# An empty indirect gather on GpSimd ahead of the first tile's gather, in an attention and routed-expert kernel

## What is computed

```python
x = x + xattn(layernorm(x), ctx)     # 16 heads of 16, keys from context and x, causal on x
x = x + ffn(layernorm(x))

def ffn(x):                          # T = 2048 tokens, E = 8 experts, cap = T // E
    probs = softmax(xt @ Wg)
    _, top_idx = top_k(probs.T, cap)             # each expert takes its 256 best tokens
    # a token taken by several goes to the best of these, one taken by none to its best expert
    tok2exp = where(assigned, argmax(masked), argmax(probs.T))
    for e in range(E):
        out += where(tok2exp == e, weight, 0) * (gelu(xt @ W1[e]) @ W2[e])
```

## Time and profile before

| | us |
|---|---|
| median of three runs | 372.68 (372.06 to 373.13) |
| the profiled execution | 371.51 |
| its span, first to last instruction | 369.5 |
| TensorE busy | 350.9 |
| ScalarE busy | 264.4 |
| VectorE busy | 207.4 |
| GpSimd busy | 126.3 |
| mean granted TensorE clock | 0.993 of full |

### The profile page before, as it was taken

The page is one execution under the profiler, slowest core; times in us unless marked ns, Lnnn a source line. Parts: engine busy times, 40 slices in busy tenths (PEclk is TensorE's granted clock), DMA queues, the critical chain, the costliest instruction groups (busy, mean ns, idle before and its releaser), DMA issues.

```text
span 369.5 us, 11056 instructions
## 1 busy us (share of the span) xinstructions
PE 350.9 (95%) x4371; PEld 224.8 (61%) x4371; DVE 207.4 (56%) x711; ACT 264.4 (72%) x386; POOL 126.3 (34%) x222
## 2 busy tenths in 40 slices
PE   8999999999999999999999999998786799999995
PEld 7757547444434444444434344787665799999994
DVE  4999797454546455454635456697785233333332
ACT  3675564999999999999999999307851445555440
POOL 6445768001010313131120306504404346555523
PEclk9999999999999999999999999999999899999999
DMA  7634899505366563826565125401652321323200
GB/s 246 192 106 138 248 249 324 175 4 150 73 197 159 186 171 92 249 45 179 129 180 126 35 35 182 134 2 64 217 179 63 103 86 58 110 70 93 70 26 33
DMA packets 37374, 47.83 MB, mean 129 GB/s; under 512 B 8780, under 2 KB 26626, under 8 KB 37313
## 3 DMA queue, kind: packets, MB, share of 16 engines
q1 hardware_dynamic: 34368, 40.26, 37.3%
q0 software_dynamic: 2608, 6.43, 5.6%
q10 hardware_dynamic: 337, 0.32, 0.3%
HBM read 32.84 MB, written 13.81 MB: 126 GB/s over the span
## 4 chain that ended last, share of the span: by engine, by line
PE 79%; ACT 9%; DVE 7%; issue 3%; POOL 1%; POOLq 0%; ACTq 0%
PE ps L1189 20%; PE ps L1165 18%; PE ps L1412 10%; PE ps L1426 9%; PE ps L1143 8%; ACT pbuf L912 7%; PE ps L1089 4%; DVE stats L1794 1%; PE ps L1058 1%; ACT v_st L962 1%; PE ps L1400 1%; DVE xe L1789 1%; PE ps L1282 1%; POOL pbuf L789 1%; PE ps L1072 1%
## 5 line engine op out<-in xcount | busy, mean ns | idle before, releaser
L912 ACT ACTIVATE pbuf<-ps 128x948 f32<-128x948 f32 (+2 forms) x192 | 167.5, 1028 | 0.1
L1758 DVE SCALAR_TENSOR_TENSOR pbuf<-pbuf,seen 128x128 f32<-128x128 f32 (+1 forms) x256 | 70.9, 309 | 65.6 <-ACT pbuf L912 64.8
L1165 PE MATMUL ps<-q_st,k_st 98*32 98x512 bf16 (+4 forms) x1920 | 100.0, 328 | 1.5 <-ACT pbuf L912 1.4
L1189 PE MATMUL ps<-pbuf,v_st 128*32 128x512 f32 (+4 forms) x1024 | 96.4, 472 | 0.0
L1165 PEld LDWEIGHTS ps<-q_st,k_st 98*32 98x32 bf16 x1920 | 46.8, 96 | 68.5 <-issue 27.2
L1412 PE MATMUL ps<-mid,piece_f 128*128 128x128 f32 x320 | 40.5, 281 | 4.0 <-issue 4.0
L758 POOL TENSOR_TENSOR mid<-mid 64x256 f32<-64x256 f32 x28 | 20.3, 752 | 69.0 <-DVE pbuf L1751 50.9
L1412 PEld LDWEIGHTS ps<-mid,piece_f 128*128 128x128 f32 x320 | 40.2, 198 | 5.1 <-issue 4.2
L1189 PEld LDWEIGHTS ps<-pbuf,v_st 128*32 128x32 f32 x1024 | 27.3, 109 | 25.3 <-issue 10.5
L1426 PE MATMUL ps<-pbuf,mid 128*128 128x256 f32 (+1 forms) x168 | 37.7, 369 | 0.0
L999 ACT ACTIVATE mid<-ps 128x512 f32<-128x512 f32 x20 | 11.9, 597 | 34.8 <-issue 18.0
(11 more groups left out here) (274 smaller groups left out, 388.0 us busy)
## 6 DMA issues: line engine op xcount, KB each, us to landing
wts<-in_L_ffn_W SPq DMA_DIRECT2D x16, 512.0 KB, 5.6
k_st<-k_cut SPq DMA_DIRECT2D x48, 147.2 KB, 3.3
q_st<-q_cut SPq DMA_DIRECT2D x48, 128.0 KB, 3.2
q_cut<-wts SPq DMA_DIRECT2D x8, 384.0 KB, 4.6
k_cut<-wts SPq DMA_DIRECT2D x8, 384.0 KB, 4.9
token_rows<-xe SPq DMA_DIRECT2D x4, 512.0 KB, 4.4
mid<-mid SPq DMA_DIRECT2D x28, 64.0 KB, 2.5
mid<-reciprocals SPq DMA_DIRECT2D x28, 64.0 KB, 2.3
```

The source lines that it names most:

```text
L912: nc.scalar.activation(pbuf[:, s % 2, r, c0:end], st_ps[(s * GH + r) % NST][:, c0:end], ACT.Exp, scale=SCALE).then_inc(exp_done, 1)
L1165: last = nc.tensor.matmul(st_ps[(s * GH + r) % NST][c:c + 32, a:z], k_st[pa][:, r, t * P + c:t * P + c + 32], q_st[pa][:, r, q0 + a - c0:q ...
L1189: last = nc.tensor.matmul(o_ps[32 * r:32 * r + 32, a:z], v_st[pa][:, t, r, :], pbuf[:, s % 2, GH - 1 if t == SHORT else r, a + dc:z + dc], ...
L1758: last = nc.vector.scalar_tensor_tensor(a, a, 3.0e38, seen[:, off:off + w], ALU.min, ALU.mult)
```

## The change

GpSimd fills an index column `no_rows` with one number, 4096, which is above the bound of 4095 (`pair_end`), right at the beginning of the routing's constants. After the wait for `rows_sent` it issues one more indirect gather with it, of the form of L805, into `y_sb[0]`. All 128 indices are above the bound. The real gather of tile 0 follows as before. VectorE, ahead of tile 0's L2013, which is the first to write `y_sb[0]`, waits in addition for the empty gather's signal `none_in`.

```diff
+        none_made = sem("none_made")
+        none_in = sem("none_in")
...
+        no_rows = sb("no_rows", [P, 1], U32)
...
             pool.wait_ge(pv_done, 2 * NG * NSTEP + 2)
+            nc.gpsimd.iota(no_rows[:, :], pattern=[[0, 1]], base=T * XW // D, channel_multiplier=0).then_inc(none_made, 1)
             nc.gpsimd.memset(r_one, 1.0).then_inc(route_made, 1)
...
             pair_end = pool.to_reg(T * XW // D - 1)
             token_end = pool.to_reg(T - 1)
+            pool.wait_ge(none_made, 1)
             pool.wait_ge(rows_sent, 16 * 2 * (TT // 4))
+            pool.sem_inc(index_there, 1)
+            pool.indirect_dma_start(y_sb[0], None, rows_d.rearrange("t (h d) -> (t h) d", d=D),
+                                    bass.IndirectOffsetOnAxis(no_rows[:, 0:1], 0),
+                                    bounds_check=pair_end, oob_is_err=False).then_inc(none_in, 16)
             pool.sem_inc(index_there, 1)
             pool.wait_ge(first_done, 1)
             pool.indirect_dma_start(first_x, None, rows_d.rearrange("t (h d) -> (t h) d", d=D),
...
                 if k >= RING:
                     v.wait_ge(sent[k % RING], 16 * (k // RING))
+                if k == 0:
+                    v.wait_ge(none_in, 16)
                 if lasts:
```

## The result

The kernel after took 375.31 us, the median of four runs (374.37 to 376.06), against 372.6 (372.06 to 373.13, four runs) for the kernel before: a ratio of 1.0085 [1.0061, 1.0109], slower by 2.7 us. The forecast was 372.6 with a range to 374.0, so it was wrong in sign and outside its range. The profiled execution of the kernel after took 374.37 us with a span of 372.4 (before: 371.51 and 369.5).

The account below looks back on a forecast made before the run. TensorE, busy 95% of 369.5 us, bounds the kernel, so only its idle or slowed time counts. Sum 0 + 0 + 0 - 0.1 + 0 on the median 372.68 gives 372.6 us; range 366.8 to 374.0.

Parts of the forecast that it names:

- What bounds the kernel now: Whole kernel: TensorE busy 95% of 369.5 us; 4.02 us idle after L1400's transposes; late tile 0 rows cost at most 0.2 us.
- the stand: TensorE issuing nothing for 4.02 us between L1400's transposes and the expert matmuls at 288.73; taken as unchanged.
- The iota, the cover, the added wait: Iota in GpSimd's 15.13 us idle, dummy gather from 276.9 to 278.2 in idle time, VectorE's `none_in` wait: all cost nothing.
- VectorE beside the dummy (C): VectorE's routing steps beside the dummy: taken as nothing, ends 0 and 1.25 us; rival C, VectorE blocked, 373.9 us, chance 0.05.
- The first gather itself: L805 on GpSimd, 1253 ns against 1000: gain between 0 and 0.25 us, TensorE can use 0.2; taken 0.1.
- D: Rival at the first gather: the dummy warms nothing, not cold or cools again; 372.7 us, inside the forecast's 0.61.
- What is late next is unchanged: the copies L994 and L1993 and with them the 4.02 us: After the transposes: the two copies of the transposed tile and TensorE's 4.02 us idle stay as they were.
- A: After the first transposes: the 4.02 us belong to the indirect queue's first use and vanish; 367.2 us, chance 0.23.
- B: At `slots_ready` after L1379: the stall comes twice, the dummy's completion at 280.1 holding TensorE's signal; 376.5 us, chance 0.08.
- a shifted burst that lengthens the stand: At the gathers after tile 0's: a shifted burst lengthens the 4.02 us by over 1.1 us; chance 0.03.

Follow-up runs that it names:

- two empty gathers: Kernel after with a second empty gather, into `y_sb[1]`, and `none_in` awaited at 32: 375.2 us, kernel before 373.03 (one run each).
- late job: Group of runs in which the kernel before took 372.6 to 373.3 us and showed TensorE's late signal; in the other five groups it took 366.3 to 366.8.
- the hold: Kernel before with tile 2's gather and those after it waiting for TensorE's first transposes (`fx_ready`): 366.89 us against 366.25; elsewhere 366.65 against 373.3.
- the hold on the kernel after: Kernel after with all gathers behind tile 1's held until TensorE's first signal: 369.08 us, 0.9918 [0.9881, 0.9955] against the kernel before.

## Why the prediction was wrong, step by step

*What bounds the kernel now*: right as a reading. It found the stand, its length, its nameless releaser and the clock after it.

*The iota, the cover, the added wait*: right. The empty gather lies in the idle time, and `first_tok` is not late. The gather began at 277.52, not 276.9, as 0.82 us of "issue" stand before it, and took 1.50 us, outside the 1.0 to 1.29 of its nearest rows, so it ended at 279.0 and not by 278.2. Both are hidden.

*VectorE beside the dummy (C)*: nothing, as taken. From L1970 (L1961 of before) to `first_tok` VectorE needs 3.00 us in both kernels, with the empty gather in the middle of them or without. By the prediction's reading of the Trainium skill, SBUF — State Buffer, "Who interferes with whom", a block of up to 1.25 us could have stood here; none is seen.

*The first gather itself*: the gain was 0.25 us of GpSimd and about 0.18 of TensorE, where 0.1 was taken and 0 to 0.2 bounded. The half of it that blamed VectorE's presence was wrong: the five VectorE operations lie beside the 1.00 us too. In the twenty traces the first gather took 1.25 us without an empty one ahead, 0.99 to 1.01 with one. It is coldness, and D is wrong.

***What is late next is unchanged: the copies L994 and L1993 and with them the 4.02 us***: this is the step that failed. The copies are what is late next, but the 4.02 us is no constant that follows the transposes at a fixed distance. It became 6.8 us, and the sum lacked these 2.8 us. The prediction read it as a wait and asked whether it would vanish (A) or be there twice (B). It did not ask what feeds it. The text even had a case with this outcome, a shifted burst that lengthens the stand, and gave it 0.03 and no price, outside the range; that the shift is the cause is not shown, and two empty gathers speak against it. With A at 0.23, so with a real doubt about where the stand comes from, a change just ahead of its cause deserved as much on the long side as on the short one. The view that would have told more was the raw semaphore record: `fx_ready` updated 3.8 us after its matmul had ended.

*A*: wrong. The first use of the queue was moved 3 us ahead and the stand stayed. *B*: wrong. The empty gather landed at 280.1, just where B wanted it, and the signal of `slots_ready` came then too, 14 ns after its matmul; that B's 376.5 is near the measured 375.3 is chance.

**What is shown and what is not.** Shown: the loss is a longer late signal (result, twice); the late signal comes and goes between jobs; with the burst thinned it goes, and with fewer small TensorE instructions nearly (one run each, the first also on the kernel after, with an interval, where part of it comes back two tiles on); SyncE's updates crawl in the same window as TensorE's (one trace). Suggested by that trace alone, and not by its time: with useless updates on another engine the late signal grows. Against the other thought, that TensorE lacks its next instructions, stands that it had run the transposes already, and that the queues moved in that stretch of the kernel before nothing but the gathers. The view of the transfers, 283 to 289 us (packets, megabytes, share of 16 engines):

```profile
q0 software_dynamic: 318, 0.96, 54.7%
```

Argued only: that it is the path of records, not of the updates themselves, that is full. The loss of records speaks for it. The Trainium skill, NOTIFIC — the notification-queue block, "7.1 Overflow: three behaviours, one of which stalls the engine", has the notification block's internal pipeline hold its producers back rather than lose a record inside; engines slowed by it would fit that, but update records missing from the trace would not. Every trace here is a recorded execution, and none could show what one without records does; the times of a late job are all long, the profiled one or not, and whether the others record as much is not known. Open are also why jobs differ, and whether the empty gather lengthens the stand by something of its own (its 16 updates, its 48 packets) or by the sooner burst. Two empty gathers, with a burst no sooner than before and a stand of 6.16, speak for the empty gather itself, and so, weakly, does the hold on the kernel after with its 369.08; against a simple sum speaks that two do no more than one. No run in a late job moves the burst alone.

**A version that beats both**: the kernel before with the hold. In a late job it took 366.65 against 373.3 (one run each), in a job that is not late 1.0002 [0.9984, 1.0020]. It takes away all but 0.44 us of the stand that the change made worse, and costs nothing that can be seen where there is none.

## What to carry to other kernels

A stand whose releaser the profile cannot name is not a constant: before leaving it in a sum unchanged, find whose signal ends it, compare that signal's time with the end of the work it reports, and price the case in which it grows. Where the signal is late against its own work, look at the load around it (indirect gathers in flight, streams of tiny instructions), and hold back transfers that nobody needs yet. Warming a queue with an empty gather buys 0.25 us of GpSimd, which pays only if the first gather's rows end the wait, and here that was 0.18 us.

## What the runs showed of the hardware that was not expected

- The first indirect gather of the kernel costs GpSimd 1.25 us, later ones 1.00; a gather in which every index is above the bound costs 1.50 as the first, 1.26 as the second. Moving no row (48 packets, 0.00 MB) is not cheaper to issue.
- The signals of TensorE's gates and first transposes were 2.4 and 3.8 us late in one job and 14 and 15 ns in another, in the same kernel; with an empty gather up to 5.1 and 6.8. An otherwise idle SyncE got 50 increments through in 10 us in that window of a late job, and one in 0.06 us once it was over.
- The traces of those jobs lack about a quarter of the gathers' update records (235 of 320 are there), while the matmuls and packets are complete, so missing records of this kind are themselves a sign.
- A gather that starts while one of VectorE's fp32 copies of 128x1024 (L2020) is running takes longer by about the rest of the copy less 0.1 us: with 0.41 us of it left 1.30 us in all, with 0.51 left 1.40 (the kernel after run again), with 0.27 left 1.16, with 0.20 left 1.07, against 1.00. The Trainium skill, SBUF — State Buffer, "Who interferes with whom", has VectorE in a 2-port mode, which such a copy can enter, block GpSimd until the instruction is over; these rows agree. The operations beside L805 are no such copies, so its 1.25 us had another cause.
